# Two graph attentions on one core: a matmul that sums a pair of heads, and a table of sums with rows twice as wide

## The reference

```python
# typed
Q, K, V = (enh @ Wq + bq), (enh @ Wk + bk), (enh @ Wv + bv)      # 4 heads of 64
scores = einsum('ehd,ehd->eh', Q[dst], K[src] + 0.2 * rel[:, None, :]) / 8
w = softmax of scores over the edges of one dst
agg = segment_sum(w[:, :, None] * V[src], dst)
x1 = layernorm(x + layernorm(agg @ Wo + bo + x) * gamma + beta)
# plain
xp = x1 @ W                                                      # 4 heads of 64
alpha = leaky_relu(a_src[src] + a_dst[dst])                      # self loops added
agg = segment_sum(softmax(alpha) * xp[src], dst)
out = layernorm(x1 + elu(agg + bias))
```

## Time and profile before

| | |
|---|---|
| median of 3 runs | 4468.4 us (4467.4 to 4470.13) |
| span of the profiled execution | 6181.0 us |
| PE busy, share of the span | 4261.5 us, 69% |
| POOL busy | 3049.7 us, 49% |
| DVE, ACT busy | 3295.8 us, 2576.2 us |
| DMA | 820553 packets, 1055.91 MB, mean 171 GB/s |

### The profile page before, as it was taken

How to read it: one execution, slowest core, us unless ns; L and a number is a source line. 1 busy time by engine, 2 the same in 40 slices (tenths; PEclk the granted TensorE clock), 3 DMA queues, 4 the chain that set the end, 5 groups by cost and what they waited for, 6 DMA issues and landing times. The chain is left out here.

```text
span 6181.0 us, 164556 instructions
## 1 busy us (share of the span) xinstructions
PE 4261.5 (69%) x50798; PEld 2746.6 (44%) x50798; DVE 3295.8 (53%) x10527; ACT 2576.2 (42%) x6781; POOL 3049.7 (49%) x3229
## 2 busy tenths in 40 slices
PE   7958878777778787778786555555555555555554
PEld 4634444444444444444443444444444443444443
DVE  3235555555555555555554455555555555555555
ACT  2323344444444444444343444444444444444444
POOL 1245555545555555555452555555555555555553
PEclk9989999999999999999997666656566566565666
DMA  7856676666666666666664555555555555555554
GB/s 224 282 163 191 185 189 186 186 186 185 186 187 183 186 186 187 185 186 186 184 185 114 145 153 156 152 151 153 152 153 153 150 152 149 154 152 152 154 150 123
DMA packets 820553, 1055.91 MB, mean 171 GB/s; under 512 B 458633, under 2 KB 632338, under 8 KB 820464
## 3 DMA queue, kind: packets, MB, share of 16 engines
q0 software_dynamic: 225072, 730.03, 42.9%
q1 hardware_dynamic: 594078, 324.02, 20.6%
q10 hardware_dynamic: 1314, 0.99, 0.1%
HBM read 919.46 MB, written 133.59 MB: 170 GB/s over the span
## 5 line engine op out<-in xcount | busy, mean ns | idle before, releaser
L766 POOL DMA_INDIRECT typed_rows<-kv,typed_index x1563 | 1491.3, 954 | 1470.8 <-remote 570.5
L1298 POOL DMA_INDIRECT plain_rows<-xp,plain_index x1563 | 1486.0, 951 | 1359.5 <-remote 536.1
L875 PE MATMUL typed_p_s<-typed_kt,typed_q 64*32 64x416 f32 x4168 | 835.7, 549 | 336.6 <-issue 289.7
L997 DVE CUSTOM_DVE_ANT_0 typed_weight<-typed_p_s,typed_far 128x416 f32<-128x416 f32 x521 | 308.3, 592 | 1113.6 <-PE typed_p_s L875 1080.8
L1400 PE MATMUL plain_p_o<-plain_rows,plain_weight_t 128*32 128x65 f32 x16672 | 630.5, 296 | 331.5 <-issue 310.7
L1433 DVE SCALAR_TENSOR_TENSOR plain_p_s<-plain_p_s,plain_a_dst,plain_damped 128x416 f32<-128x416 f32 x521 | 342.3, 657 | 865.9 <-ACT plain_damped L1553 475.1
L1389 PE MATMUL plain_p_s<-all_cst,plain_rows 128*128 128x128 f32 x2084 | 546.2, 395 | 346.0 <-issue 319.6
L1375 PE MATMUL plain_p_w<-all_cst,plain_weight 128*128 128x128 f32 x1563 | 437.5, 404 | 431.6 <-issue 286.0
L1400 PEld LDWEIGHTS plain_p_o<-plain_rows,plain_weight_t 128*32 128x32 f32 x16672 | 459.2, 154 | 556.6 <-issue 516.7
L1167 ACT ACTIVATE typed_weight<-typed_weight,typed_col 128x416 f32<-128x416 f32 x521 | 334.7, 642 | 806.6 <-issue 549.7
L1389 PEld LDWEIGHTS plain_p_s<-all_cst,plain_rows 128*128 128x128 f32 x2084 | 406.0, 210 | 463.6 <-issue 437.6
(11 more groups left out here) (191 smaller groups left out, 6936.5 us busy)
## 6 DMA issues: line engine op xcount, KB each, us to landing
typed_match<-match SPq DMA_DIRECT2D x131, 208.0 KB
plain_match<-match SPq DMA_DIRECT2D x131, 208.0 KB
agg<-qkv_zero SPq DMA_DIRECT2D x98, 264.0 KB
typed_agg<-agg SPq DMA_DIRECT2D x98, 264.0 KB
plain_agg<-agg SPq DMA_DIRECT2D x98, 264.0 KB
kv<-qkv_kv SPq DMA_DIRECT2D x98, 258.0 KB
typed_kinds<-match SPq DMA_DIRECT2D x131, 192.0 KB
typed_rows<-kv,typed_index POOLq DMA_INDIRECT x1563
```

The lines of the kernel that those rows point to most:

```text
L766: pool.indirect_dma_start(rows[:, r, j, :], None, k.kv, bass.IndirectOffsetOnAxis(ap=index[:, g, at:at + 1], axis=0)).then_inc(rows_in[r], 16)
L875: last = pe.matmul(p_s[at:at + TN, 0:SLOTS], q[own, m, :, h // 2], kt[own, h // 2, lo:lo + SLOTS], start=True, stop=True, tile_position=(H ...
L1298: pool.indirect_dma_start(rows[:, r, j, :], None, k.xp, bass.IndirectOffsetOnAxis(ap=index[:, g, at:at + 1], axis=0)).then_inc(rows_in[r], 16)
```

## The change

Both attentions: one matmul now takes the weights of a pair of heads (128 x 64) against the 130 columns of that pair, so a tile has 8 matmuls instead of 16. Of each 64 x 130 result half is useful: head 0 of a pair in the first 32 rows and the first 65 columns, head 1 in the other rows and columns. ACT copies all 130 columns into a `result` of 132 columns per partition, and in plain the maximum into two columns. `put_out` writes 528 B per partition to a table row of four heads of 132 columns for each parity. Useful in such a row are the 66-column blocks 0 and 3 of each pair; `own_sums` names these, and only they are cleared and loaded: 8 pieces of 264 B per node instead of 2 of 1056 B. The constants lose an unused pair of columns, and one 128-column part moves behind the part that is kept in SBUF.

```diff
 AG = HC + 2
+PAIR = 2 * AG
+SUMS = 2 * HEADS * AG
...
-        self.agg = dram("agg", (2, NP, HEADS, AG))
+        self.agg = dram("agg", (NP, 2, SUMS))
...
+    def own_sums(self, nodes):
+
+        return self.agg[nodes].rearrange("n a (p y c) -> n (a p) y c", p=2, y=4)[:, :, 0::3]
+
+    def tile_sums(self, parity, nodes):
+
+        return self.agg[nodes, parity].rearrange("n (h c) -> h n c", h=HEADS)
...
-        zero = z.sb("zero", [P, 2, HEADS * AG])
+        zero = z.sb("zero", [P, 2 * HEADS * AG])
...
-                sp.dma_start(k.agg[:, bass.ds(t.n * P, P)].rearrange("a n h c -> n a (h c)"), zero[:]).then_inc(zero_out, 16)
+                sp.dma_start(k.own_sums(bass.ds(t.n * P, P)), zero[:]).then_inc(zero_out, 16)
...
-        result = z.sb("result", [P, 4, AG])
+        result = z.sb("result", [P, 4, PAIR])
...
-                sp.dma_start(k.agg[t.slot(2), bass.ds(node, TN)].rearrange("n h c -> h n c"), result[:, m]).then_inc(result_out[m], 16)
+                sp.dma_start(k.tile_sums(t.slot(2), bass.ds(node, TN)), result[:, m]).then_inc(result_out[m], 16)
...
-                sp.dma_start(agg[:], k.agg[:, bass.ds(b.n * P, P)].rearrange("a n h c -> n a (h c)")).then_inc(agg_in, 16)
+                sp.dma_start(agg[:].rearrange("p a x -> p (a x)"), k.own_sums(bass.ds(b.n * P, P))).then_inc(agg_in, 16)
...
-                    for h in range(HEADS):
-                        at = TN * h
-                        last = pe.matmul(p_o[at:at + TN, 0:V], weight_t[:, t.slot(2), j * P + at:j * P + at + TN], v[:, D + V * h:D + V * h + V],
+                    for pair in range(2):
+                        at, own = HC * pair, D + 2 * V * pair
+                        last = pe.matmul(p_o[at:at + HC, 0:2 * V], weight_t[:, t.slot(2), j * P + at:j * P + at + HC], v[:, own:own + 2 * V],
                                          start=j == 0, stop=j == CH, tile_position=(0, at), skip_group_check=True)
...
-                act.copy(result[:, m, 0:V], p_o[:, 0:V]).then_inc(result_ready, 1)
+                act.copy(result[:, m].rearrange("p (y c) -> p y c", y=2)[:, :, 0:V],
+                         p_o[:, 0:2 * V].rearrange("p (y c) -> p y c", y=2)).then_inc(result_ready, 1)
...
-                act.copy(result[:, m, V:AG], col[:, m, KEEP:KEEP + 1])
-                act.copy(result[:, m, 0:V], p_o[:, t.slot(2), 0:V]).then_inc(result_ready, 1)
+                both_heads = result[:, m].rearrange("p (y c) -> p y c", y=2)
+                act.copy(both_heads[:, :, V], col[:, m, KEEP:KEEP + 1].broadcast_to((P, 2)))
+                act.copy(both_heads[:, :, 0:V], p_o[:, t.slot(2), 0:2 * V].rearrange("p (y c) -> p y c", y=2)).then_inc(result_ready, 1)
```

More of the change, by code:

```diff
@@ L69 @@
 C_ID = 0
[L70 to L73, removed]
+C_LATER = C_ID + P
+C_COVER = C_LATER + 1
 C_THIN = C_COVER + PER
@@ L86 @@
 C_CMP1 = C_PASS + G_PASSES
-C_N = C_CMP1 + 2
+C_NEG1 = C_CMP1 + 2
+C_N = C_NEG1 + P
 FAR = float(2.0 ** 50)
@@ L118, in constants @@
     c[1:, C_LATER] = 1.0
-    c[:TN, C_KEY1] = 1 + np.arange(TN)
-    c[:TN, C_KEY1 + 1] = 1.0
     c[:, C_TYPE] = p % REL
@@ L1397, in aggregate @@
                     val = rows[:, t.slot(R), j] if j < CH else rows[:, t.back(-1).slot(R), 0]
[L1398 to L1401, removed]
+                    for pair in range(2):
+                        at, own = HC * pair, 2 * V * pair
+                        last = pe.matmul(p_o[at:at + HC, t.slot(2), 0:2 * V], weight_t[:, t.slot(2), j * P + at:j * P + at + HC],
+                                         val[:, own:own + 2 * V],
                                          start=j == 0, stop=j == CH, tile_position=(0, at), skip_group_check=True)
```

## The result

The changed kernel takes 4540.31 us (median of 4 runs, 4535.53 to 4545.62) against 4469.26 us for the kernel before: ratio 1.0159, 95% interval 1.0145 to 1.0173, 71 us slower. The forecast was 4530 us, with a range of 4430 to 4630.

What follows compares the result with a forecast made beforehand. The prediction took the GpSimd gathers, 1.25 us apart, as the bound, a floor of 4395 us. To 4468 it added 42 (typed sums), 15 (clears) and 4 (loads): 4529, forecast 4530 us, range 4430 to 4630.

Steps and rivals of the forecast that it cites:

- The floor: Both attentions: 3126 gathers 1.25 us apart, 3908 us, plus 487 us outside them give 4395 us; the median is 74 above.
- The sum's length: TensorE's sum per tile: 16 passes of 130 columns in two strips take 0.43 us more, 0.87 at half clock.
- Who sees it: Typed: score waits for the sum, mean 0.32 us per tile; 3.51 becomes 3.83, 0.08 above the gathers: 42 us.
- The clears: Projection: 1024 pieces of 264 B per block cost all DMA engines 0.67 us more, 0.30 over TensorE's 2.83: 15 us.
- the prediction's signs: Listed evidence to look for, among it projection blocks of 2.83 to 3.13 us with DMA above 0.95.
- the fit: DMA packet cost, a line through two stages: 14.1 ns + 0.0369 ns per byte, giving 0.67 us per clear.
- Loads, puts and copies: Attentions: loads 4 us at the ends, otherwise hidden; puts 0.08 us of DMA; ScalarE's copy +0.06 us per tile, 0 us.
- Plain: Plain attention: TensorE's 2.77 us becomes 3.64 even at half clock, still under the gathers' 3.75: 0 us.
- The sum: Total of the terms: 4468 + 42 + 15 + 4 = 4529, forecast 4530 us.
- Hidden altogether: Rival: TensorE's longer sum fits under the gathers and the clears cost nothing, 4465 to 4477 us; chance 0.15.
- Issue decides: Rival: fewer TensorE instructions shrink the gaps before matmuls, 4395 to 4468 us, say 4420; chance 0.25.
- The DMA engines bind: Rival: DMA engines set the attentions' pace, so every packet counts, 107 us in typed and 29 in projection, 4604; chance 0.15.

Runs made afterwards that it cites:

- second profile: The kernel before, unedited, profiled once more without the long stalls of its first profiled execution: span 4463.8 us, median 4467.78 us.
- first profile: The kernel before, unedited, in the profiled execution that the prediction read, an exceptionally slow one: span 6181.0 us.
- e6_coarse: Changed kernel with clears and loads in whole pieces of 1056 B again, 256 per block of nodes; pairs, 528 B puts and 130-column copies stay: 4531.98 us.
- e10_narrow_copy: As e7_four_coarse, with ScalarE's copy of 65 columns again in both attentions, heads 1 and 3 left out: 4485.58 us.
- e7_four_coarse: As e6_coarse, with four sums of 65 columns in four strips instead of pairs, in both attentions: 4487.38 us.
- e4_after: The changed kernel again, no edit, beside the second group of runs: 4542.3 us.
- e2_wide: Changed kernel with four strips of 32 columns, 130 columns streamed through each, 32 passes instead of 16: 4558.05 us.
- e5_pairs_alone: The kernel before with only the pair matmuls of 130 columns in both attentions; copy stays at 65 columns, heads 1 and 3 left out: 4529.26 us.

## Why the prediction was right, and where its steps were not

*The floor.* Plain runs at it: 1562 gathers of 1.25 us are 1952.5 us, and the kernel before takes 1963.1. The 74 us that the prediction found above the floor (78 by the second profile) lie in typed (2019.9 - 1952.5 = 67) and plain (11), not spread over both: typed did not run at the gathers' pace, since its loop of 62.34 us is 3.90 us a tile against 3.75. So the slack of 0.24 us a tile that the prediction gave TensorE there was none. That the first profile's stalls were that execution's own is shown by the second one.

*The sum's length.* Right: 0.43 us more was forecast, 1.11 - 0.66 = 0.45 measured, and at the lower clock 1.86 us where 1.9 was forecast:

```profile
4009.18 1.86 PE L1408 MATMUL plain_p_o<-plain_rows,plain_weight_t 128*64 128x130 f32 x16
```

*Who sees it.* This step failed in its form, and its sum came near by two errors that offset each other. The prediction read the tiles behind the last gather, found +0.29 in a bare tile and +0.43 in one with block work, and set the mean of 0.32 against a mean slack of 0.24. In the last tiles TensorE does all that it does in the loop (the relation matmuls stand at 3281.65 and 3281.82 there), but the vector engine does less. In the loop it makes a comparison ahead of the add (kernel before, second profile):

```profile
1114.82 0.42 DVE L986 TENSOR_SCALAR typed_hit<-typed_kinds,all_cst 128x384 bf16<-128x384 uint8 x1
```

No tile is left to compare for at the end, so the add starts 0.33 us ahead of the sum there, and in the loop 0.01 us behind it (1115.29 and 1115.28). In the loop the add therefore covers the longer sum whole: +0. A bare tile takes 3.58 us there instead of 3.08. At the end itself the reading held: the bare tile takes 3.40 us after the change, as forecast. And the mean slack is not there: it lies in the bare tiles, while five of sixteen tiles, not three, carry block work and have none, and each grows by about 0.45. A whole loop of 16 tiles, first to last score, goes from 62.48 us (1104.95 to 1167.43) to 64.34 (1135.99 to 1200.33):

```profile
1104.95 0.90 PE L875 MATMUL typed_p_s<-typed_kt,typed_q 64*32 64x416 f32 x8 [0.26 <-issue]
...
1167.43 0.90 PE L875 MATMUL typed_p_s<-typed_kt,typed_q 64*32 64x416 f32 x8 [0.25 <-issue]
```

```profile
1135.99 0.90 PE L882 MATMUL typed_p_s<-typed_kt,typed_q 64*32 64x416 f32 x8
...
1200.33 0.90 PE L882 MATMUL typed_p_s<-typed_kt,typed_q 64*32 64x416 f32 x8
```

That is 1.86 us, where five tiles by 0.45 would make 2.25; the bare ones gave 0.4 back. Over 521/16 loops it is 61 us, typed's 60. The term charged at 42 us measured 60; that it came so near is luck, since the two errors have nothing to do with each other.

*The clears.* The mechanism was right and the size high for the DMA time, near for the result. SP's queue in the rows above: 56.40 MB in 200 us at 2.83 us a block are 70.7 blocks, 0.897 x 200/70.7 = 2.54 us of all engines each; after the change 70.7 x 55.17/56.40 = 69.1 blocks, 2.89 us each. That is 0.35 us more, where 0.67 was forecast, and just above TensorE's 2.83. The blocks follow one another every 2.90 us, and the share is 0.96, both as the prediction's signs had it. The term of 15 us measured 8.1 to 10.7 in four runs and 26 in one group of three, within its bound of 29.

By the page that the prediction weighed here, the Trainium skill, DMA: Bandwidth & Descriptors, Why small descriptors are slow, the estimate was 0.21 us and nothing on the path; the trace puts it between that and the fit.

*Loads, puts and copies.* The loads' 4 us at the two ends became 5.6 us between the stages and -0.2 at the end; whole pieces give back only 0.7 of the first, so the loads' cut is not its cause. The pairs on the old table have 3.0 of it (79.9 against 76.9); the rest stays open. Hidden in the middle they are, as forecast (e6_coarse). ScalarE's copy, answering to the earlier trace rows, reads 276 ns where 0.27 us was forecast, and the width costs at most 2 us (e10_narrow_copy against e7_four_coarse):

```profile
L1181 ACT COPY typed_result<-typed_p_o 128x130 f32<-128x130 f32 x521 | 144.0, 276 | 81.3 <-PE typed_p_o L896 71.9 <-issue 1.9
```

The puts were charged nothing in time: right for the change as a whole, but without the pairs the wide rows cost 15 us, for which the prediction had no mechanism.

*Plain* was forecast at nothing and shows -2 to +6 us.

*The sum.* Beside one another in one group of runs: pairs alone 4529.26 - 4472.06 = 57 us, the wide table with whole pieces 3 more (e6_coarse), the finer clears and loads 10 more (e4_after), 70 together; forecast were 42, nothing, and 15 + 4. No run beat the kernel before.

*The rivals.* "Hidden altogether" failed where it was doubted, in the tiles without slack. "Issue decides" is refuted by e2_wide: twice the passes and weight loads at the same width take the same time. "The DMA engines bind" is refuted for typed by e5_pairs_alone, which has the whole loss there without a further piece; what is left for it is the projection.

## What to carry to other kernels

Price a merged matmul by the columns that each strip of the array streams in turn, useless ones included: joining two heads of 65 into 130 halved the instructions and nearly doubled the time, because four strips had worked side by side. Slack is a property of a kind of tile: read it for each place of the steady loop, not as a mean, and not from the last tiles, in which one of the engines has less to do. Finer DMA pieces cost where the engines are nearly full; here 10% of room was not enough for cutting 264 of a block's 778 KB into four times the pieces.

## What the runs showed of the hardware

The granted clock in plain, a mean of its two levels 1.2 and 2.4 GHz, was 0.77 before and 0.87 after, with TensorE busy for 1123.65 and 1214.25 us of 1750. So in all profiles from the second on: the seven whose plain sums stream 130 columns have 0.925 to 0.932 over the whole span, the six with 65 columns 0.875 to 0.886. Where the packets' time filled the DMA engines, the same kernel's projection ended at 357.7 us in one group of runs and 375.2 in another, while the kernels with whole pieces stayed within 349.6 and 351.7. SP's issue of a clear took longer too, and that not for the number of pieces alone: 383 ns before, then the changed kernel, then e10_narrow_copy, which has 256 pieces as before, but in rows twice as wide.

```profile
L571 SPq DMA_DIRECT2D agg<-qkv_zero x98: 606/627/1019, 33.8 to 323.2; - x98
```

```profile
L575 SPq DMA_DIRECT2D agg<-qkv_zero x98: 540/561/1718, 33.8 to 315.7; - x98
```

In e10_narrow_copy it is hidden: the first gather comes at 351.0 us. Whether it is hidden in the changed kernel is not shown.
